# Blocks of x stored from ScalarE's queue, and the second unit's scores moved into the next pair, in a cross-attention and expert-FFN kernel

## Chip, core and metric

One core of one Trainium2 chip runs the whole program in one launch. The metric is the device time of one execution, in microseconds (us); lower is better. TensorE is PE, VectorE DVE, ScalarE ACT, GpSimd POOL and SyncE SP.

## What is computed

x has 32 sequences of 64 tokens with 512 features, 2048 tokens in all; the context has the same shape. Everything is float32.

```python
def attention(query, kv, Wq, bq, Wkv, bkv, Wo, bo):      # 32 query heads, 8 key/value heads, head width 128
    q = (query @ Wq + bq).reshape(B, L, 8, 4, 128)
    k, v = split(kv @ Wkv + bkv, 2, axis=-1)
    scores = einsum('blkgd,bmkd->bkglm', q, k) / sqrt(128)
    o = einsum('bkglm,bmkd->blkgd', softmax(scores), v)
    return o.reshape(B, L, 4096) @ Wo + bo
x = x + attention(layernorm(x), ctx, ...)
x = x + experts(layernorm(x))      # 8 experts of rank 16, the two best per token, softmax gates
```

## The kernel before

**Precision.** A float32 operand is split into a high part (a rounded copy, written by ACT) and a low part (the rest, a subtraction on POOL or DVE). A matrix product is three passes, high x high, low x high and high x low, on lines 1408 to 1410. So a high part always waits on ACT and a low part on POOL or DVE, before PE can use it.

**Start.** Keys and values of all heads are made in four steps. A step has 8 value tiles `V` and 8 key tiles `K`; PE fills a ring of four PSUM banks, DVE moves each tile to one of three slots (`SLOTS`) in `parts`, with a wait for the slot's earlier store, and SP stores it to `values_dram` or `keys_dram`. Between them PE transposes tiles of the context and of the normalised x. From x, ACT, DVE and POOL make seven blocks of 1 MB (`OPS`), which are operands of a seven-product scheme for x Wq (Strassen's, in Winograd's form), for each of two halves of the tokens, called duos 0 and 1 here. The blocks stand in `xo`, seven places, and `store_blocks` writes them to `x_dram`: duo 1's after step 1's first keys, duo 0's after step 3's, both from SP's queue, among the stores of keys. The stores share one counter, `blocks_stored`.

**Main part.** 16 pairs of units, `duo(g, p, first)`: for each of 8 key/value heads g, p = 0 and 1. A unit is 512 tokens for the four query heads of g. Per pair PE does 14 products (`product(g, p, k, r)`, six matmuls of 512 columns each, in the order k = 1, 6, 2, 7, 4, 5, 3), which DVE adds up to four tiles of queries (`y_sum`, `z_sum`, `w_sum`, `query_sum` for c11, c21, c22, c12); `scores` of both units, in chunks of four sequences; the softmax of each chunk, which goes to and fro: copy out of PSUM (ACT, `copy_half`), add and turn (DVE, `s_add`, `s_max`), peak swap (ACT, `swap_max`; DVE, `s_peak`), subtraction (POOL, `shift`), exponential (ACT), sum (DVE, ACT), scaling (POOL), turn back (DVE, `p_turn`), split (ACT, POOL). Then `outputs` (probabilities x values), and `out` (times Wo, added to `y`). `outputs` and `out` of a pair's units are done in the next pair. Pairs 2 to 13 are a hardware loop. Each engine's order is written out by hand in its own `duo`; engines meet at semaphores only.

**Places of blocks.** In the main part a pair's seven blocks share four places of `xo` (`BUF_OF`), because places 4 to 6 hold `oT` and `pT`, attention's own tiles. Before the first product of a block, PE waits for its load, `block_loaded`. SP issues `load_block(p, op, used)` when product `used` has released the place. In the first pair, blocks 4 to 6 are loaded again into places 2, 0 and 1. Blocks that the next pair needs first are loaded at the end of a pair.

**The first pair's joins.** ACT's `first_product` writes product 1 into `parts`, whose places were the stores' slots, so it waits until the last three stores of keys have landed. PE's first product waits until DVE has emptied the last key tile. `bo_bc`, the bias of the output, lies in `k_raw` until POOL's `residual` has added it to all 16 tiles of `y`; the first load of keys waits for that.

## Time and profile before

| what | value |
|---|---|
| median of 3 runs | 1111.5 us (1110.66 to 1112.6) |
| profiled execution's own time | 1111.75 us |
| its span in the trace | 1109.5 us |
| PE busy | 1045.1 us, 94% |
| DVE, POOL, ACT busy | 806.4, 675.6, 557.0 us |
| mean granted PE clock | 0.974 |

The time holds 2.25 us outside the span. Busy time of PE counts a matmul from its start to its modelled end. A granted clock of 1.00 is 2.4 GHz and 0.50 is 1.2 GHz.

### The profile page before, as it was taken

The page shows a single profiled execution, that of the slowest core. Times are in us where ns is not written, and L with a number is a line of the kernel's source. Part 1 is how long each engine was busy: PE and PEld are TensorE (multiplying, and loading weights), DVE is VectorE, ACT ScalarE, POOL GpSimd, SP SyncE. Part 2 cuts the span into 40 slices and gives each one's busy share as a digit, 9 for nine tenths or more (in the row PEclk, how much of TensorE's full clock was granted, in tenths as well). Part 3 has the DMA queues.
Part 4 walks back from the last instruction along what each step waited for, and adds up shares of the span by engine and source line. Part 5 has one row for each costly group of instructions (what it writes and reads, how often), then busy time and mean ns, then how long its engine had stood idle before and what let it go on. Part 6 is the DMA issues. An engine that isn't in the chain of part 4 may idle for free.

```text
span 1109.5 us, 17269 instructions
## 1 busy us (share of the span) xinstructions
PE 1045.1 (94%) x5389; PEld 856.0 (77%) x5389; DVE 806.4 (73%) x1420; ACT 557.0 (50%) x1314; POOL 675.6 (61%) x563
## 2 busy tenths in 40 slices
PE   7999799784999999999999999999999999997996
PEld 5887687664887887888788788878887888886884
DVE  4462346346897797789878877977887797788795
ACT  3132103225665665567566656756666665664320
POOL 1275125746786677578667867776786677674210
PEclk9999899986999999999999999999999999998998
DMA  8647753884727456372736446282736546240013
GB/s 303 191 123 277 235 180 105 328 299 149 294 93 259 145 201 233 113 286 92 284 127 222 179 170 240 101 299 102 261 122 228 182 167 243 102 149 10 1 40 113
DMA packets 86040, 201.12 MB, mean 181 GB/s; under 512 B 10560, under 2 KB 43368, under 8 KB 70384
## 3 DMA queue, kind: packets, MB, share of 16 engines
q1 hardware_dynamic: 86000, 200.61, 51.4%
q8 instruction: 23, 0.38, 0.1%
q14 instruction: 17, 0.14, 0.0%
HBM read 164.93 MB, written 35.65 MB: 181 GB/s over the span
## 4 chain that ended last, share of the span: by engine, by line
PE 58%; POOL 15%; DMA 9%; issue 8%; DVE 7%; SPq 1%; ACT 1%; POOLq 0%; DVEq 0%; ACTq 0%
PE banks L1408 17%; PE banks L1409 16%; PE banks L1410 16%; DMA xo<-x_dram 5%; POOL w_l L555 4%; DMA keys_dram<-parts 3%; PE banks L1543 3%; POOL qT_l L555 2%; POOL xo L555 2%; POOL low_or_x L588 2%; POOL low_or_x L581 2%; PE banks L1526 2%; PE banks L1527 2%; PE banks L1433 2%; SPq L411 1%
## 5 line engine op out<-in xcount | busy, mean ns | idle before, releaser
L555 POOL TENSOR_TENSOR qT_l<-parts,qT_h 128x512 fp32r<-128x512 f32 x128 | 165.3, 1296 | 63.6 <-ACT qT_h L725 63.5
L1408 PE MATMUL banks<-wo_h,xo 128*128 128x512 f32 x512 | 203.8, 398 | 0.0
L1409 PE MATMUL banks<-wo_l,xo 128*128 128x512 f32 x512 | 199.9, 391 | 0.0
L1410 PE MATMUL banks<-wo_h,xo 128*128 128x512 f32 x512 | 199.5, 390 | 0.0
L1408 PE MATMUL banks<-xo,w_h 128*128 128x512 f32 x448 | 181.4, 405 | 14.2 <-DVE parts L1008 11.0
L1409 PE MATMUL banks<-xo,w_h 128*128 128x512 f32 x448 | 177.3, 396 | 0.0
L1410 PE MATMUL banks<-xo,w_l 128*128 128x512 f32 x448 | 175.8, 393 | 0.0
L555 POOL TENSOR_TENSOR xo<-sT,xo 128x512 fp32r<-128x512 f32 (+1 forms) x72 | 102.2, 1420 | 76.9 <-ACT xo L725 76.9
L969 DVE TENSOR_TENSOR xo<-banks,xo 128x512 fp32r<-128x512 f32 (+1 forms) x156 | 100.7, 665 | 27.4 <-ACT xo L725 26.7
L1117 DVE SCALAR_TENSOR_TENSOR parts<-banks,g_bias,parts 128x512 f32<-128x512 f32 x128 | 95.0, 742 | 34.2 <-PE banks L1410 30.6
L588 POOL TENSOR_TENSOR low_or_x<-low_or_x,row_sum 128x512 f32<-128x512 f32 x64 | 70.7, 1104 | 74.3 <-DVE row_sum L1153 74.3
L1408 PEld LDWEIGHTS banks<-xo,w_h 128*128 128x128 f32 x448 | 85.2, 190 | 38.9 <-issue 17.0
L1408 PEld LDWEIGHTS banks<-wo_h,xo 128*128 128x128 f32 x512 | 96.1, 188 | 23.0
L1410 PEld LDWEIGHTS banks<-wo_h,xo 128*128 128x128 f32 x512 | 96.1, 188 | 20.9
L1409 PEld LDWEIGHTS banks<-wo_l,xo 128*128 128x128 f32 x512 | 96.2, 188 | 18.3
L725 ACT ACTIVATE qT_h<-parts 128x512 fp32r<-128x512 f32 x128 | 80.6, 630 | 58.5 <-DVE parts L1117 56.7
L725 ACT ACTIVATE xo<-banks 128x512 fp32r<-128x512 f32 (+1 forms) x156 | 85.0, 582 | 43.4 <-PE banks L1543 22.4
L1164 DVE TENSOR_TENSOR y<-banks,y 128x512 f32<-128x512 f32 x120 | 81.4, 683 | 33.5 <-PE banks L1410 33.0
L1410 PEld LDWEIGHTS banks<-xo,w_l 128*128 128x128 f32 x448 | 85.1, 190 | 19.0
L1409 PEld LDWEIGHTS banks<-xo,w_h 128*128 128x128 f32 x448 | 85.2, 190 | 15.4
L581 POOL TENSOR_TENSOR low_or_x<-low_or_x,row_max 128x512 f32<-128x512 f32 x64 | 70.5, 1101 | 42.7 <-DVE row_max L1139 41.9
L813 ACT COPY low_or_x<-banks 64x512 f32<-64x512 f32 x64 | 37.3, 583 | 116.5 <-PE banks L1527 116.4
(142 smaller groups left out, 2282.4 us busy)
## 6 DMA issues: line engine op xcount, KB each, us to landing
xo<-x_dram SPq DMA_DIRECT2D x108, 1024.0 KB, 6.9
x_dram<-xo SPq DMA_DIRECT2D x14, 1024.0 KB, 12.9
raw<-in_L_xattn_Wkv_dram SPq DMA_DIRECT2D x8, 1024.0 KB, 6.4
values_dram<-parts SPq DMA_DIRECT2D x64, 128.0 KB, 2.5
keys_dram<-parts SPq DMA_DIRECT2D x32, 256.0 KB, 2.8
raw<-in_L_xattn_Wq_dram SPq DMA_DIRECT2D x8, 1024.0 KB, 5.5
k_raw<-keys_dram SPq DMA_DIRECT2D x32, 256.0 KB, 4.7
raw<-in_L_xattn_Wo_dram SPq DMA_DIRECT2D x8, 1024.0 KB, 5.4
```

Of the source, the lines that this page charges most:

```text
L555: return nc.gpsimd.tensor_tensor(dst, src, high_part.bitcast(F32), ALU.subtract)
L581: nc.gpsimd.tensor_tensor(s[:, blocks, :], s[:, blocks, :], row_max[:, blocks].unsqueeze(2).broadcast_to([P, D // QR, QR]), ALU.subtract). ...
L588: nc.gpsimd.tensor_tensor(s[:, blocks, :], s[:, blocks, :], row_sum[:, blocks].unsqueeze(2).broadcast_to([P, D // QR, QR]), ALU.mult).then ...
L725: return nc.scalar.activation(dst, src, ACT.Copy)
L813: act.copy(half[L:P, c], att_s[L:P, :, 0, :])
L969: return nc.vector.tensor_tensor(dst, src, high_part.bitcast(F32), ALU.subtract)
L1117: nc.vector.scalar_tensor_tensor(out=slot_of(c, r), in0=product_of(d, p, k, r), scalar=q_bias(c, r), in1=slot_of(what, r), op0=ALU.add, op ...
L1164: nc.vector.tensor_tensor(y[:, t, :], ring[:, slot, :], y[:, t, :], ALU.add).then_inc(y_added, 1)
L1408: mm(dst, stat[0], mov[0], start=start, stop=False)
L1409: mm(dst, stat[0], mov[1], start=False, stop=False)
L1410: return mm(dst, stat[1], mov[0], start=False, stop=stop)
L1543: last = mm(turn[:, i, n % 2 * G * L:(n % 2 + 1) * G * L], v[keys_of, n, :], p[keys_of, n, :], start=p is pT_h and v is v_h, stop=p is pT_l)
```

## The change

Five edits, most of them for the pairs 0 and 1 only.

1. `store_blocks` moves from SP to ACT. Duo 1's seven stores are issued behind `split_wv(2)` in the start's order, duo 0's behind `split_q(0)`.
2. Pair 0 uses its seven blocks where they were made. SP no longer waits for the stores at its start, and loads none of blocks 4 to 6 for it; the wait for all 14 stores comes before the loads for pair 1. ACT waits for the stores before it writes `pT`.
3. `bo_bc` lies in `v_raw`. The first load of keys no longer waits for the residuals; the first load of values does, and POOL does tiles 3 and 7 later, inside pair 0.
4. The scores of pair 0's second unit move from its end into pair 1, on PE behind products 6 and 2. `outputs(0, ...)` move back behind product 4. On DVE the sums y of pair 1 move ahead to pair 0's end, and the second unit's softmax moves behind the sums c11 of pair 1. On ACT, `first_product` of pair 1 and `keys_high(1)` are moved ahead.
5. In all pairs with p = 0, the load of Wo (`load_wo`) is issued behind the loads of blocks 5, 4 and 6 and of the keys; before, it stood ahead of blocks 4 and 6.

```diff
@@ -186,7 +186,7 @@
         x_copy = parts[:, 5, :].rearrange("p (c n) -> p c n", c=KC)
-        bo_bc = k_raw.rearrange("p b l -> p (b l)")
+        bo_bc = v_raw.rearrange("p n d -> p (n d)")
         sT = sb("sT", [P, 2 * D])
@@ -402,13 +402,6 @@
                 load_w(step, wkv_v, NKV * HD + step % CHUNKS * D)
-
-            def store_blocks(duo, pairs_done):
-
-                sp.wait_ge(diff_low, pairs_done)
-                sp.wait_ge(tile_emptied, tile_no["x", DUO_TILES[pairs_done - 1][1]] + 1)
-                for op in range(OPS):
-                    sp.dma_start(x_dram[duo, op], xo[:, op].rearrange("p s k n -> p (s k n)").bitcast(F32)).then_inc(blocks_stored, 16)
@@ -437,10 +430,6 @@
                             load_w(STEPS, wq_v, 0)
-                        if name[1] == 1:
-                            store_blocks(1, 4)
-                        if name[1] == STEPS - 1:
-                            store_blocks(0, 8)
                 if name[0] == "c" and 4 <= name[1] < PTILES:
@@ -490,18 +479,16 @@
                 if first:
-                    sp.wait_ge(blocks_stored, 16 * DUOS * OPS)
+                    for m in range(len(kv_order) - SLOTS, len(kv_order)):
+                        sp.wait_ge(kv_stored[m % SLOTS], kv_value[m])
                 else:
                     load_values(g if p else g - 1, 2 * p - 1 if p else UNITS - 1, 2 * d - 1)
-                load_block(p, 5, product(1))
+                    load_block(p, 5, product(1))
+                    load_block(p, 4, product(6))
+                    load_block(p, 6, product(2))
+                load_keys(g, 2 * p + 1, 2 * d + 1)
                 if p == 0:
                     load_wo(wo_v[:, bass.ds(g * G, G), :], QLOWS + OPS * g + OPS)
-                load_block(p, 4, product(6))
-                if first:
-                    for m in range(len(kv_order) - SLOTS, len(kv_order)):
-                        sp.wait_ge(kv_stored[m % SLOTS], kv_value[m])
-                load_block(p, 6, product(2))
-                load_keys(g, 2 * p + 1, 2 * d + 1)
                 if p == 1 and last_group:
@@ -512,16 +499,19 @@
                     load_w(STEPS + g + 1, wq_v, (g + 1) * (G * HD))
+                if first:
+                    sp.wait_ge(blocks_stored, 16 * DUOS * OPS)
                 if not last:
...
                     load_block(1 - p, 2, product(5))
+                if first:
+                    sp.wait_ge(resid_ready, TILES)
                 load_values(g, 2 * p, 2 * d)
...
-            sp.wait_ge(resid_ready, TILES)
             m = kv_no["K", 0, 0, 0]
@@ -642,6 +632,9 @@
                 query_low(d, "c11", 1)
+                if first:
+                    residual(3)
+                    residual(7)
                 query_low(d, "c21", 0)
@@ -698,7 +691,7 @@
             split_q(0, list(USE_OF), True)
-            for t in (0, 4, 1, 5, 2, 6, 3, 7):
+            for t in (0, 4, 1, 5, 2, 6):
                 residual(t)
@@ -765,6 +758,13 @@
+            def store_blocks(duo, pairs_done):
+
+                act.wait_ge(diff_low, pairs_done)
+                act.wait_ge(tile_emptied, tile_no["x", DUO_TILES[pairs_done - 1][1]] + 1)
+                for op in range(OPS):
+                    act.dma_start(x_dram[duo, op], xo[:, op].rearrange("p s k n -> p (s k n)").bitcast(F32)).then_inc(blocks_stored, 16)
+
             def first_product(d, p, r):
@@ -841,9 +842,13 @@
                 wo_high_part(0)
-                first_product(d, p, 0)
-                keys_high(2 * d)
-                first_product(d, p, 1)
+                if second:
+                    copy_half(1, 1)
+                    keys_high(2)
+                else:
+                    first_product(d, p, 0)
+                    keys_high(2 * d)
+                    first_product(d, p, 1)
                 if not first:
@@ -878,6 +883,8 @@
                 copy_half(2 * d, 1)
+                if first:
+                    keys_high(1)
                 swap_max(2 * d, 0)
@@ -885,12 +892,17 @@
                 exponents(2 * d, 0)
-                keys_high(2 * d + 1)
+                if not first:
+                    keys_high(2 * d + 1)
                 if not first:
...
                 exponents(2 * d, 1)
+                if first:
+                    first_product(1, 1, 0)
+                    first_product(1, 1, 1)
+                    act.wait_ge(blocks_stored, 16 * DUOS * OPS)
                 if split:
@@ -900,7 +912,7 @@
                 probs_high(2 * d, 1)
-                if not last:
+                if not first and not last:
                     copy_half(2 * d + 1, 1)
@@ -918,7 +930,10 @@
                         split_wv(name[1] + 1)
+                    if name[1] == 1:
+                        store_blocks(1, 4)
             split_q(0, list(USE_OF), True)
+            store_blocks(0, 8)
             duo(0, 0, True)
@@ -1183,15 +1199,21 @@
                     s_peak(2 * d - 1, 0)
-                y_sum(d, p, 0)
-                if not first:
-                    s_max(2 * d - 1, 1)
-                y_sum(d, p, 1)
-                if not first:
-                    s_sum(2 * d - 1, 0)
-                    s_peak(2 * d - 1, 1)
+                if not second:
+                    y_sum(d, p, 0)
+                    if not first:
+                        s_max(2 * d - 1, 1)
+                    y_sum(d, p, 1)
+                    if not first:
+                        s_sum(2 * d - 1, 0)
+                        s_peak(2 * d - 1, 1)
                 query_sum(d, p, "c11", 0)
                 query_sum(d, p, "c11", 1)
+                if second:
+                    s_add(1, 1)
+                    s_max(1, 1)
+                    s_sum(1, 0)
+                    s_peak(1, 1)
                 if not first:
@@ -1253,12 +1275,15 @@
                     combine_w(g + 1, 4, False)
+                if first:
+                    y_sum(1, 1, 0)
+                    y_sum(1, 1, 1)
                 s_add(2 * d + 1, 0)
...
                 add(7)
-                if not last:
+                if not first and not last:
                     s_add(2 * d + 1, 1)
@@ -1479,12 +1504,10 @@
                 first, second = isinstance(d, int) and d == 0, isinstance(d, int) and d == 1
-                buf = BUF_OF[op]
+                buf = op if first else BUF_OF[op]
                 if r == 0:
-                    if op >= XBUFS:
-                        pe.wait_ge(block_loaded[buf], d * 32 + 16)
-                    elif not first:
-                        pe.wait_ge(block_loaded[buf], d * 16 if buf == 3 else d * 32)
+                    if not first:
+                        pe.wait_ge(block_loaded[buf], d * 32 if op >= XBUFS else d * 16 if op == 3 else d * 32 - 16)
                     if p == 0:
@@ -1563,16 +1587,24 @@
                 product(g, p, 6, 1)
-                if not first:
+                if second:
+                    scores(0, 1, 0)
+                elif not first:
                     outputs(2 * d - 2, 0)
...
                 product(g, p, 2, 1)
+                if second:
+                    scores(0, 1, 1)
                 product(g, p, 7, 0)
...
                 product(g, p, 4, 0)
-                if not first:
+                if second:
+                    outputs(0, 0)
+                elif not first:
                     outputs(2 * d - 2, 1)
                 product(g, p, 4, 1)
+                if second:
+                    outputs(0, 1)
                 product(g, p, 5, 0)
@@ -1589,10 +1621,12 @@
                 out(5)
-                scores(d, 1, 0)
+                if not first:
+                    scores(d, 1, 0)
                 out(6)
                 out(7)
-                scores(d, 1, 1)
+                if not first:
+                    scores(d, 1, 1)
```

What the edits do to the engines' orders is seen in three places. First SP, in step 1 of the start: one piece of the difference in SP's rows. `keys_dram<-parts` are the stores of keys, `x_dram<-xo` those of the blocks, `raw<-in_L_xattn_Wkv_dram` a load of weights.

```order
 L401 DMA keys_dram<-parts 128x512 x2
 L376 DMA raw<-in_L_xattn_Wkv_dram 128x4x512
-L411 DMA x_dram<-xo 128x2048 x7
 L401 DMA keys_dram<-parts 128x512 x6
 L388 DMA y<-in_x_dram 128x512 x4
```

ACT in the same step, after the change. `w_h<-raw` is `split_wv(2)`, `qT_h<-banks` are high parts of context tiles 8 to 13, `wo_h<-raw` the next split of weights.

```order
L718 ACTIVATE w_h<-raw 128x512 x4
L766 DMA x_dram<-xo 128x2048 x7
L718 ACTIVATE qT_h<-banks 128x4x128 x6
L718 ACTIVATE wo_h<-raw 128x512 x4
L718 ACTIVATE qT_h<-banks 128x4x128 x2
```

The seven stores left SP's row, where six stores of keys stood behind them, and stand on ACT ahead of the context tiles.

Second SP in pair 0, before the change. `k_raw<-keys_dram` loads keys, `raw<-in_L_xattn_Wo_dram` is `load_wo`, `xo<-x_dram` loads blocks, `v_raw<-values_dram` values.

```order
L411 DMA x_dram<-xo 128x2048 x7
L401 DMA keys_dram<-parts 128x512 x6
L468 DMA k_raw<-keys_dram 128x512
L480 DMA xo<-x_dram 128x2048
L380 DMA raw<-in_L_xattn_Wo_dram 128x4x512
L480 DMA xo<-x_dram 128x2048 x2
L468 DMA k_raw<-keys_dram 128x512
L480 DMA xo<-x_dram 128x2048 x2
L475 DMA v_raw<-values_dram 64x4x128 x2
L480 DMA xo<-x_dram 128x2048 x2
L468 DMA k_raw<-keys_dram 128x512
```

And after it:

```order
L401 DMA keys_dram<-parts 128x512 x6
L457 DMA k_raw<-keys_dram 128x512 x2
L380 DMA raw<-in_L_xattn_Wo_dram 128x4x512
L469 DMA xo<-x_dram 128x2048 x2
L464 DMA v_raw<-values_dram 64x4x128 x2
L469 DMA xo<-x_dram 128x2048 x2
L457 DMA k_raw<-keys_dram 128x512
```

The three loads of pair 0's own blocks 5, 4 and 6 are gone, and both units' keys come ahead of every block.

Third DVE in pair 1, before the change: the two sums y (L1094), the softmax of unit 1's second chunk (L1132, L1134) and sum of its first (L1145), the sums c11 (L1117), the low parts of unit 0's first outputs (L969), and then the sums z (L1102).

```order
L1094 TENSOR_TENSOR parts<-banks,parts 128x512
L1132 STREAM_TRANSPOSE low_or_x<-sT 128x512
L1134 TENSOR_REDUCE row_max<-low_or_x 128x16
L1094 TENSOR_TENSOR parts<-banks,parts 128x512
L1145 TENSOR_REDUCE row_sum<-low_or_x 128x16
L1139 TENSOR_TENSOR row_max<-row_max,other 128x16
L1117 SCALAR_TENSOR_TENSOR parts<-banks,g_bias,parts 128x512 x2
L969 TENSOR_TENSOR xo<-banks,xo 128x2x4x64 x2
L1150 TENSOR_TENSOR row_sum<-row_sum,other 128x16
L1153 RECIPROCAL row_sum<-row_sum 128x16
L1102 TENSOR_TENSOR parts<-banks,parts 128x512 x2
```

After it, with the lines' new numbers (L1132 is `query_sum`, L1141 and L1142 `s_add`, L984 the low parts of outputs, L1117 z):

```order
L1132 SCALAR_TENSOR_TENSOR parts<-banks,g_bias,parts 128x512 x2
L1141 TENSOR_TENSOR sT<-banks,low_or_x 64x512
L1142 TENSOR_TENSOR sT<-banks,low_or_x 64x512
L1147 STREAM_TRANSPOSE low_or_x<-sT 128x512
L1149 TENSOR_REDUCE row_max<-low_or_x 128x16
L1160 TENSOR_REDUCE row_sum<-low_or_x 128x16
L1154 TENSOR_TENSOR row_max<-row_max,other 128x16
L984 TENSOR_TENSOR xo<-banks,xo 128x2x4x64 x2
L1165 TENSOR_TENSOR row_sum<-row_sum,other 128x16
L1168 RECIPROCAL row_sum<-row_sum 128x16
L1117 TENSOR_TENSOR parts<-banks,parts 128x512 x2
```

The addition of the second chunk's halves stood at pair 0's end and now stands between c11 and z, and the sums y left for pair 0's end.

## Rows read from the trace of the kernel before

**Rows 1.** The page: PE's busy share, and its granted clock in 40 slices.

```profile
PE 1045.1 (94%) x5389; PEld 856.0 (77%) x5389; DVE 806.4 (73%) x1420; ACT 557.0 (50%) x1314; POOL 675.6 (61%) x563
...
PEclk9999899986999999999999999999999999998998
```

**Rows 2.** Waits of the whole span, PE's: total us, times, longest.

```profile
PE banks L1408 <- DVE parts L1008: 11.0, 1, 11.0
PE banks L1433 <- DVE qT_l L969: 10.9, 2, 10.2
```

**Rows 3.** Stretches: length, busy of PE, PEld, DVE, ACT, POOL, clock, DMA, GB/s.

```profile
100.00:110.00 10.00, 8.42 (x41) 6.60 (x39) 0.69 (x1) 2.92 (x6) 9.77 (x8) 1.00 1.00 424
...
220.00:230.00 10.00, 3.15 (x8) 2.51 (x9) 2.88 (x4) 0.00 (x0) 7.48 (x7) 0.50 0.81 282
```

**Rows 4.** Timeline of SP's queue: start, length in us, then what it issued.

```profile
92.85 4.72 SPq L411 DMA_DIRECT2D x_dram<-xo  x7
97.61 23.09 SPq L401 DMA_DIRECT2D keys_dram<-parts  x6
...
202.87 6.61 SPq L411 DMA_DIRECT2D x_dram<-xo  x7
```

**Rows 5.** DMA of 80 to 130 us: times issued, size, median us to landing.

```profile
x_dram<-xo SPq DMA_DIRECT2D x7, 1024.0 KB, 13.9
keys_dram<-parts SPq DMA_DIRECT2D x8, 256.0 KB, 3.3
```

**Rows 6.** Timelines of ACT, DVE and PE around the first stall, idle time in brackets.

```profile
99.04 2.20 ACT L725 ACTIVATE w_h<-raw 128x512 fp32r<-128x512 f32 x4 [9.94 <-DMA raw<-in_L_xattn_Wkv_dram]
...
105.70 0.60 ACT L725 ACTIVATE qT_h<-banks 128x512 fp32r<-128x512 f32 x1 [2.61 <-PE banks L1433]
...
117.08 0.75 DVE L1008 TENSOR_SCALAR parts<-banks,bias 128x512 f32<-128x512 f32 x1 [14.64 <-DMA keys_dram<-parts]
...
118.58 1.09 PE L1433 MATMUL banks<-ident,y 128*128 128x128 f32 x4 [10.16 <-DVE qT_l L969]
```

**Rows 7.** The chain that ended last, one step a row, behind the first stall.

```profile
119.66 0.43 PE banks L1408
...
123.15 0.23 PE banks L1408
```

**Rows 8.** Timeline of PE, the last key product and the waits in pairs 0 and 1.

```profile
215.43 0.39 PE L1410 MATMUL banks<-qT_h,wo_l 128*128 128x512 f32 x1
...
226.85 0.76 PE L1408 MATMUL banks<-xo,w_h 128*128 128x512 f32 x1 [11.03 <-DVE parts L1008]
...
251.66 0.36 PE L1526 MATMUL banks<-qT_h,kT 128*128 128x256 f32 x1 [1.39 <-DVE sT L1127]
...
260.65 0.55 PE L1526 MATMUL banks<-qT_h,kT 128*128 128x256 f32 x1 [7.81 <-POOL kT L555]
...
267.46 0.55 PE L1526 MATMUL banks<-qT_h,kT 128*128 128x256 f32 x1 [4.75 <-DVE sT L1127]
...
286.87 0.39 PE L1408 MATMUL banks<-xo,w_h 128*128 128x512 f32 x1
```

**Rows 9.** Timeline of ACT: last weight split, pair 0's copies and keys, last exponential.

```profile
211.64 0.63 ACT L725 ACTIVATE w_h<-sT 128x512 fp32r<-128x512 f32 x1
230.80 0.59 ACT L773 COPY parts<-banks 128x512 f32<-128x512 f32 x1 [18.52 <-DMA keys_dram<-parts]
232.15 0.63 ACT L725 ACTIVATE kT<-k_raw 128x512 fp32r<-128x512 f32 x1 [0.77 <-DMA k_raw<-keys_dram]
...
261.59 0.63 ACT L823 ACTIVATE low_or_x<-low_or_x 128x512 f32<-128x512 f32 x1 [0.84 <-POOL low_or_x L581]
```

**Rows 10.** Waits of PE from 320 to 1060 us.

```profile
PE banks L1408 <- DMA xo<-x_dram: 2.7, 6, 0.5
```

**Rows 11.** Timeline of SP's queue in pair 2.

```profile
328.70 0.41 SPq L380 DMA_DIRECT2D raw<-in_L_xattn_Wo_dram  x1
329.61 0.81 SPq L480 DMA_DIRECT2D xo<-x_dram  x2
```

More of the change, by code:

```diff
@@ L832, in duo @@
                 split, last = p == 1 and not last_group, p == 1 and last_group
+                second = isinstance(d, int) and d == 1
                 def wo_high_part(c):
@@ L1175, in duo @@
                 split, last = p == 1 and not last_group, p == 1 and last_group
+                second = isinstance(d, int) and d == 1
                 def add(j):
@@ L1549, in duo @@
                 d = g * DUOS + p
+                second = isinstance(d, int) and d == 1
                 def out(j):
```

## The prediction

> **What bounds the kernel now.** I read the page first. PE is busy 94% of the span, no other engine over 73%, so only time in which PE stands still, or runs at the lower clock, can be won. The row of granted clock is 9 in nearly all slices and dips in two places, at about 110 and 220 to 280 us [rows 1]. The list of PE's waits names them: 11.0 us for DVE's eviction at L1008, and 10.2 us for DVE's low part of a context tile [rows 2]. Stretches of 10 us show what goes on there: DMA is full, 424 GB/s, and then PE stands at clock 0.50 [rows 3]. SP's queue says what fills it: seven stores of x blocks from 92.85 us and seven from 202.87, each time with the key stores behind them [rows 4]. A block store lands after 13.9 us, a key store usually after 3.3 [rows 5]. Behind the blocks DVE waits 14.64 us for a slot, and PE 10.16 for DVE [rows 6]. So both large stalls are of one kind: a small store behind 7.34 MB in the same queue, 17.2 us at 427 GB/s.
>
> Between pairs 0 and 1 PE waits for other things: 1.39, 7.81 and 4.75 us for scores of pair 0, whose softmax and keys have no other matmuls to hide behind [rows 8]. In the loop only six waits for a block are left, 2.7 us [rows 10].
>
> **First place: stores of step 1.** PE lost 10.16 us [rows 6] and ran on at half clock: seven steps of the chain take 0.43 us in place of 0.23, 1.4 us, and the four transposes ahead of them 0.6 more [rows 7]. That is 12.2 us. Now the key stores don't stand behind the blocks. What is new is that ACT issues. Its weight split ends at 101.24 [rows 6], and seven issues took SP 4.72 us [rows 4], so ACT is free at 105.96. High part 0.60 and low part 0.69 of the first context tile end at 107.3. PE wanted to turn the third tile, which needs that bank, at 105.07 (its high part began at 105.70, behind 0.60 of transposes [rows 6]): a new wait of 2.3. No row shows what an issue costs on ACT. Below, it is nothing, and the wait too; above, 6.61 us as SP's second time [rows 4], and the wait is 4.2. I take SP's first, since that queue was empty too. Value stores and the next weight load then run beside the blocks up to about 125 us. PE has a ring of four banks and DVE three slots between; I allow 0.7, with 0 and 3 as ends. Gain 12.2 - 2.3 - 0.7 = **9.2** (5 to 12.2).
>
> **Second place: stores of step 3, pairs 0 and 1.** I count from the last key product's end, 215.82, to product 5 of pair 1 at 286.87, 71.0 us [rows 8]. In it PE does 24 products of six matmuls at 0.2285 (1.37 each, 32.9), four score chunks of 1.0 and two `outputs` of 0.95: 38.8. Waits are 11.03, 0.48 (a block), 1.39, 7.81 and 4.75, 25.5 together. The rest, 6.7, is low clock behind them.
>
> Now the same stretch anew, by durations from the trace. DVE empties the last key tile at 216.7: 1.0 wait. Four products run to 222.4. Product 2 needs ACT's copy of product 1, and that the last key store. Before, copy, keys and copy ran from 230.80 to 233.26, 4.1 us behind that store's eviction [rows 9]. Now the blocks share the DMA engines with it, so I add 1 to 2 us; the first load of keys comes behind it and must land before ACT reaches the second copy, about 226.3. PE's second half of product 2 would start at 223.8: **2.5** (0 to 5). Eight more products bring the scores of chunk 0 at 237.3; POOL, with two residuals of 1.23 in between, has the low parts at 236.0, no wait. Chunk 1 waits for `s_add` of chunk 0 as before, 1.4, and ends at 242.1. Stores of blocks, from 212.3 [rows 9], need 17.2 us plus some 2.4 MB of other transfers, so they are done at about 235; block 0 of pair 1 lands at about 241.5. It is just in time.
>
> Then pair 1, in its new order. Products 1 and 6 end at 247.6. Scores of unit 1 need the keys' low part, which POOL does behind shift and c12: 248.8, **1.3**. Product 2 needs the copy on ACT, now behind the second exponential. Before, that ended at 262.22 [rows 9], 9.4 us behind chunk 1's end at 252.84; keys are split earlier now, so 8.5, and the copy is there at 251.2: **1.3**. Chunk 1 of unit 1 waits for `s_add`, behind an inverse and two sums y on DVE: **2.7**. Product 4 waits 0.3 for c11. The second `outputs` waits until DVE has the first's low parts, which now stand behind `s_add`, `s_max`, sum and peak of unit 1, with two turns to ACT between them: 267.9, **3.5**; z is 0.8 behind. New waits: 1.0 + 2.5 + 1.4 + 1.3 + 1.3 + 2.7 + 0.3 + 3.5 + 0.8 = 14.8. 38.8 + 14.8 = 53.6, against 71.0: 17.4 won. PE's next scores then wait 1.3 more for POOL's c21. Gain **16.1**; the chain's joints of 1 to 3 us each, and the copy's bounds, give 9 to 22.
>
> **Third place: load of Wo.** In pair 2 it went out at 328.70, when `w_l` was finished, and blocks 4 and 6 behind it, at 329.61 [rows 11]. Product 6 had released block 4's place at about 326. Now block 4 goes 3 us earlier and the wait of 0.40 to 0.50 in each of six pairs is gone, **2.6** (2 to 2.7). Wo goes out at about 331, and is wanted 39 us later: covered. The other waits of SP move with it; keys are out at 331 as before. If Wo were to collide with blocks 0 and 2 at 336, it costs nothing, since they are wanted in the next pair.
>
> **Free.** The bias in `v_raw`: the values' load now waits for POOL's last residual at 233, and is issued behind blocks at 236. Wait for all stores on ACT: 235 against 251.
>
> **Sum.** 9.2 + 16.1 + 2.6 = 27.9. From the profiled execution's 1111.75 (span 1109.5 and 2.25 around it) that leaves 1083.9, and 1083.6 from the median, which is 0.25 lower.
>
> **A rule against it.** Rows 4 and 5 show small stores late behind large ones of one queue; they can't show two queues. The Trainium skill, page "DMA: Bandwidth & Descriptors", section "Issuing engines are not separate DMA queues", says that transfers started by several engines run on the same 16 DMA engines, and that spreading saves issue time only. Its section "Queues, rings and completion order" gives SP and ACT a ring each on every DMA engine, served in turn by the packet. No run here shows either yet. By the second, the sum stands; by the first, read strictly, it is the first rival.
>
> **Rivals.** *One line for both queues* (12%). Key stores issued behind the blocks still land behind them. In step 1 they mostly don't matter: the blocks now go out at 101 rather than 93, and three slots and a ring of four carry PE until 119, so the 9.2 stay. At pair 0, the last key store would land at 231, the second copy be done at 234.5, and PE would lose 8 us and 2 of clock more: 1093.6. For it: 13.9 us for each block at full bandwidth [rows 5]. Against it: nothing yet.
>
> *ACT is held until the blocks have gone* (4%). An issue then takes 2.4 us, ACT stays until 118 and 229. The first place loses 2 in place of winning 9, the second wins 10: 1101. Against it: SP issued seven in 4.72 us while they took 17 to move [rows 4].
>
> *The waits of pair 1 don't come* (8%), as engines make up for them: 14.8 shrinks to 5, and the first place gives all 12.2. Together with the loop's 2.6 that is 40.7: 1071.
>
> *Slower* (3%): low clock throughout pairs 0 and 1. The new waits are many and short, where the old were few and long. If PE were granted 1.2 GHz from 242 to 292 us, each of its 180 matmuls costs 0.43 in place of 0.23 [rows 7]: 36 us, more than the 27.9, for 1120. It turns to a loss from 140 matmuls on. Against it: the clock came back within 12 matmuls after 226.85, and a wait of 1.39 at 251.66 [rows 8] was followed by full clock.
>
> **Numbers.** The forecast has 70%; 3% are for something that undoes the gain elsewhere. The likeliest case's own bounds give gains from 5 + 9 + 2 = 16 to 12.2 + 22 + 2.7 = 37, 1075 to 1095. The range, 1072 to 1098, takes in the first rival and the edge of the third, and leaves out the other 15 in 100. A measurement of this kernel tells 0.2% from no change. Chances: faster 0.93, within 0.2% 0.03, slower 0.04.
>
> **What would show it.** PE's waits at L1408 for DVE and at the context tile fall from 11.0 and 10.2 to under 4 each. The key stores land within 6 us while blocks are under way. ACT shows a gap of about 5 us ahead of the first context tile of step 2. No wait for a block in pairs 2 to 12. Pair 1 has five or six waits of 1 to 4 us ahead of product 5. I am wrong if key stores land after 10 us or more, if block 0 of pair 1 comes late by over 3 us, or if the granted clock stays low past 245 us.

## The result, and the profile after

| what | before | after |
|---|---|---|
| median in one group of runs | 1112.05 us (1110.66 to 1113.71, 4 runs) | 1094.24 us (1093.7 to 1095.01, 4 runs) |
| ratio to before, 95% interval | 1 | 0.984 (0.9823 to 0.9857) |
| span of the profiled execution | 1109.5 us | 1092.8 us |
| mean granted PE clock | 0.974 | 0.983 |

The changed kernel is 17.8 us faster; the forecast was 27.9 faster, 1083.6. The time lies in the range (1072 to 1098), and direction and places are as forecast. Of three terms the middle one is much too large. Of the 10.6 us to the forecast, 0.5 come from the median before, 1112.05 where the forecast started from 1111.5. (One more group of runs, e12 below, gave 1095.88 for the same kernel: between groups, differences are uncertain by some 1.6 us.)

The page of the changed kernel, its busy row, its row of granted clock, and the queues. q1 is SP's, q10 is new and ACT's.

```profile
PE 1044.5 (96%) x5389; PEld 856.2 (78%) x5389; DVE 805.2 (74%) x1420; ACT 556.5 (51%) x1314; POOL 674.9 (62%) x563
...
PEclk9999999898999999999999999999999999998998
...
q1 hardware_dynamic: 83552, 182.78, 48.4%
q10 hardware_dynamic: 2016, 14.68, 3.3%
```

Against [rows 1] PE's work is the same 1045 us; what was won is idle time. In the row of clock the dip at 110 us has gone; that at 220 to 280, an 8 and a 6 before, is now an 8 at 191 to 219 and an 8 at 246 to 273 us.

**First place.** Timelines of ACT and PE there: start, length, engine, line, what; idle time and its releaser in brackets.

```profile
100.79 5.12 ACTq L766 DMA_DIRECT2D x_dram<-xo  x4
105.96 1.08 ACT L718 ACTIVATE qT_h<-banks 128x512 fp32r<-128x512 f32 x2 [5.33 <-issue]
...
128.35 2.19 ACT L718 ACTIVATE wo_h<-raw 128x512 fp32r<-128x512 f32 x4 [10.06 <-DMA raw<-in_L_xattn_Wkv_dram]
...
107.43 0.63 PE L1458 MATMUL banks<-ident,y 128*128 128x128 f32 x4 [1.66 <-DVE qT_l L984]
...
131.80 0.50 PE L1433 MATMUL banks<-w_h,qT_h 128*128 128x512 f32 x1 [2.25 <-DVE qT_l L984]
```

ACT stands 5.33 us issuing, as forecast, and PE waits 1.66 in place of 10.16 [rows 6]. The second row of PE is new: PE waits 2.25 us at 131.80, since the weights of the next step land late. SP issued them only at 117.68, behind the key stores and four loads of x tiles that ran beside the blocks; the blocks themselves had gone by 122.

**Second place.** Timelines of PE, DVE, ACT and SP's queue from the last key product to product 5 of pair 1, to set beside [rows 8, 9]. L1023 empties key tiles, L773 copies product 1.

```profile
208.19 0.39 PE L1435 MATMUL banks<-qT_h,wo_l 128*128 128x512 f32 x1
213.72 0.77 PE L1433 MATMUL banks<-xo,w_h 128*128 128x512 f32 x1 [5.15 <-DVE parts L1023]
...
223.87 0.47 PE L1433 MATMUL banks<-xo,w_h 128*128 128x512 f32 x1 [2.12 <-ACT parts L773]
227.32 0.50 PE L1433 MATMUL banks<-xo,w_h 128*128 128x512 f32 x1 [1.82 <-ACT parts L773]
242.23 0.35 PE L1549 MATMUL banks<-qT_h,kT 128*128 128x256 f32 x1 [1.40 <-DVE sT L1142]
251.72 0.36 PE L1549 MATMUL banks<-qT_h,kT 128*128 128x256 f32 x1 [2.83 <-issue]
...
253.91 0.77 PE L1433 MATMUL banks<-xo,w_h 128*128 128x512 f32 x1 [1.01 <-ACT parts L773]
270.37 0.58 PE L1566 MATMUL banks<-xo,v_h 64*128 64x256 f32 x2 [2.97 <-DVE xo L984]
272.26 0.77 PE L1433 MATMUL banks<-xo,w_h 128*128 128x512 f32 x1 [0.25 <-DVE parts L1117]
...
212.83 0.75 DVE L1023 TENSOR_SCALAR parts<-banks,bias 128x512 f32<-128x512 f32 x1 [6.11 <-DMA keys_dram<-parts]
...
204.44 6.95 ACTq L766 DMA_DIRECT2D x_dram<-xo  x7
223.14 0.59 ACT L773 COPY parts<-banks 128x512 f32<-128x512 f32 x1 [18.14 <-DMA keys_dram<-parts]
226.16 0.63 ACT L718 ACTIVATE kT<-k_raw 128x512 fp32r<-128x512 f32 x1 [2.44 <-DMA k_raw<-keys_dram]
...
213.98 14.60 SPq L457 DMA_DIRECT2D k_raw<-keys_dram  x2
```

From the last key product's end, 208.57, to product 5 at 272.26 are 63.7 us, in place of 71.0. The waits sum to 17.6, the work is the same 38.8, and 7.3 are left, nearly all of it for matmuls at 1.2 GHz (durations of 0.77 and 0.63 in place of 0.39). Three waits at the front, 9.1 us, hang on transfers: DVE can't empty the last key tile until a slot's store has landed, ACT can't copy until the last key store has, and ACT's second copy stands behind the keys, landed at 226.1. No row shows a wait for a block.

What the two queues moved in that stretch, 206 to 222 us: each queue's packets, MB and share of the 16 engines' time; then times issued, size, median us to landing.

```profile
q10 hardware_dynamic: 749, 5.48, 84.5%
q1 hardware_dynamic: 575, 1.05, 17.2%
...
x_dram<-xo ACTq DMA_DIRECT2D x5, 1024.0 KB, 13.3
keys_dram<-parts SPq DMA_DIRECT2D x3, 256.0 KB, 10.3
k_raw<-keys_dram SPq DMA_DIRECT2D x1, 256.0 KB, 12.2
```

**Loop.** The copy of a group's bias on DVE stands once in each pass of two pairs; the first and the sixth after it, in the changed kernel.

```profile
310.67 0.17 DVE L1198 COPY g_bias<-bias 128x4 f32 x1
...
902.59 0.17 DVE L1198 COPY g_bias<-bias 128x4 f32<-128x4 f32 x1
```

### The profile page after: what moved, and what is told of

The parts are those of the page before. It is cut to its first block, busy times and chain, and to the rows that moved or that the text cites. A ratio compares the mean times of both kernels' runs of the same rounds, so it can differ in the third digit from the quotient of the medians.

```text
span 1092.8 us, 17254 instructions
## 1 busy us (share of the span) xinstructions
PE 1044.5 (96%) x5389; PEld 856.2 (78%) x5389; DVE 805.2 (74%) x1420; ACT 556.5 (51%) x1314; POOL 674.9 (62%) x563
## 4 chain that ended last, share of the span: by engine, by line
PE 83%; DVE 6%; DMA 5%; ACT 2%; POOL 2%; issue 1%; SPq 1%; ACTq 1%; DVEq 0%
PE banks L1433 25%; PE banks L1434 23%; PE banks L1435 23%; PE banks L1566 5%; PE banks L1550 3%; PE banks L1549 3%; DMA raw<-in_L_xattn_Wkv_dram 2%; PE banks L1458 1%; DMA k_raw<-keys_dram 1%; DMA keys_dram<-parts 1%; DMA raw<-in_L_xattn_Wq_dram 1%; ACTq L766 1%; SPq L388 0%; POOL wo_l L545 0%; DVE stats L1059 0%
## 5 line engine op out<-in xcount | busy, mean ns | idle before, releaser
L984 DVE TENSOR_TENSOR xo<-banks,xo 128x512 fp32r<-128x512 f32 (+1 forms) x156 | 100.7, 665 | 28.7 <-ACT xo L718 28.1
L1132 DVE SCALAR_TENSOR_TENSOR parts<-banks,g_bias,parts 128x512 f32<-128x512 f32 x128 | 94.9, 742 | 30.3 <-PE banks L1435 27.9
L1435 PEld LDWEIGHTS banks<-xo,w_l 128*128 128x128 f32 x448 | 85.7, 191 | 19.2
```

What stands on the lines that cost most here:

```text
L984: return nc.vector.tensor_tensor(dst, src, high_part.bitcast(F32), ALU.subtract)
L1132: nc.vector.scalar_tensor_tensor(out=slot_of(c, r), in0=product_of(d, p, k, r), scalar=q_bias(c, r), in1=slot_of(what, r), op0=ALU.add, op ...
L1435: return mm(dst, stat[1], mov[0], start=False, stop=stop)
```

## The experiments

Every kernel was timed in turns with the kernel before. Medians of the kernel before were 1111.88 us (e1 to e4), 1110.61 (e5 to e8) and 1111.94 (e9 to e12).

**e1, late stores.** The changed kernel, with pair 0's seven stores issued on ACT behind its two copies of product 1:

```diff
                     first_product(d, p, 1)
+                    if first:
+                        store_blocks(0, 8)
...
             split_q(0, list(USE_OF), True)
-            store_blocks(0, 8)
```

> The kernel after the change, with pair 0's seven block stores issued on ACT behind pair 0's two copies of product 1, so that the last key stores and the first load of keys no longer run beside them. Sharing theory (small transfers are served in turn with the 8 KB rows of the blocks and land after about 10 us in place of 3.5, and this sets PE's start of pair 0): the last key store lands within 4 us, the waits of 5.15, 2.12 and 1.82 us at pair 0's products shrink to under 3 together and product 2 starts 8 us sooner; block 0 of pair 1 then comes some 4 us late, so the net gain is 3 to 6 us, 1088 to 1091. Clock theory (what the second place lost is the granted clock of 0.5 after each wait): waits may move but low clock stays, 1093 to 1095.

Measured 1088.35 us (1087.53 to 1090.22), ratio 0.9791 (0.9775 to 0.9807). DMA from 200 to 232 us, and PE's waits:

```profile
keys_dram<-parts SPq DMA_DIRECT2D x4, 256.0 KB, 2.5
raw<-in_L_xattn_Wo_dram SPq DMA_DIRECT2D x1, 1024.0 KB, 19.2
...
209.36 0.47 PE L1434 MATMUL banks<-xo,w_h 128*128 128x512 f32 x1 [1.01 <-DVE parts L1024]
...
229.67 0.58 PE L1550 MATMUL banks<-qT_h,kT 128*128 128x256 f32 x1 [2.36 <-POOL qT_l L545]
...
242.79 0.80 PE L1434 MATMUL banks<-xo,w_h 128*128 128x512 f32 x1 [7.08 <-DMA xo<-x_dram]
```

The three front waits shrink from 9.1 to 1.0 us, with key stores landing in 2.5 us: the blocks beside them made the waits. Product 2's second half begins 7.9 us behind the last key product, in place of 18.75. About half of these 10.8 us is given back (5.8 are left at the first pass's bias copy): PE waits 2.36 us for POOL, and since the stores now end later, pair 1's block 0 comes 7.08 us late.

**e2, filled wait.** The changed kernel with 22 matmuls on idle data ahead of pair 0's first product:

```diff
             pe.wait_ge(diff_low, 8)
+            for _ in range(22):
+                mm(turn[:, 0, :], wo_h[:, 0, 0:P], cT[0][0][:, 0, :], start=True, stop=True)
             duo(0, 0, True)
```

> The kernel after the change, with 22 extra matmuls of 512 columns (5.0 us at full clock) into a free bank, in the wait ahead of pair 0's first product; their result is never read. They keep PE busy so that the granted clock stays high. Clock theory: pair 0's first 16 matmuls run at 0.23 in place of 0.43 us each, 3.4 us won, 1091. Sharing theory: the copy of product 1 waits for the last key store whatever PE does, so the products only wait longer at product 2: same as the change, 1094 within 1.

Measured 1094.61 us (1093.29 to 1095.72), ratio 0.9848 (0.9832 to 0.9865): nothing. The first products ran at full clock (granted 1.00 from 206 to 214 us), and then PE waited for the copy, 4.37 us in place of 2.12:

```profile
222.62 0.76 PE L1433 MATMUL banks<-xo,w_h 128*128 128x512 f32 x1 [4.37 <-ACT parts L773]
```

**e3, spread stores.** The changed kernel with duo 1's seven stores issued one each behind context tiles 8 to 14.

```diff
                 if name[0] in "cx":
                     tile_high(name)
+                    if name[0] == "c" and 8 <= name[1] < 8 + OPS:
+                        store_blocks(1, 4, [name[1] - 8])
...
-                    if name[1] == 1:
-                        store_blocks(1, 4)
```

> The kernel after the change, with duo 1's seven stores issued one by one on ACT, each behind the high part of one of the context tiles 8 to 14, in place of seven in a row. Sharing theory: ACT no longer stands 5.3 us ahead of the first context tile, small stores meet fewer blocks, and PE's waits of 1.66 and 2.25 us go: 2 to 4 us won, 1090 to 1092. Rival (the order of the tiles' splits, not the stores, sets these waits): 1094.

Measured 1094.12 us (1091.19 to 1096.34), ratio 0.9832 (0.9814 to 0.985): nothing either. ACT no longer stands, the 1.66 us are gone, but the next weights come only 1.1 us sooner than in the changed kernel, and PE waits for them, 3.89 us where the two waits made 3.91:

```profile
127.26 0.63 ACT L718 ACTIVATE wo_h<-raw 128x512 fp32r<-128x512 f32 x1 [11.70 <-DMA raw<-in_L_xattn_Wkv_dram]
...
130.70 0.80 PE L1433 MATMUL banks<-w_h,qT_h 128*128 128x512 f32 x1 [3.89 <-DVE qT_l L984]
```

**e4, Wo's load alone.** The kernel before with edit 5 only (`load_wo` behind `load_keys` for p = 0).

```diff
                 load_block(p, 5, product(1))
-                if p == 0:
-                    load_wo(wo_v[:, bass.ds(g * G, G), :], QLOWS + OPS * g + OPS)
                 load_block(p, 4, product(6))
...
                 load_keys(g, 2 * p + 1, 2 * d + 1)
+                if p == 0:
+                    load_wo(wo_v[:, bass.ds(g * G, G), :], QLOWS + OPS * g + OPS)
```

> The kernel before the change with the fifth edit alone, Wo's load behind the loads of blocks 5, 4 and 6 and of the keys. If only the wait for block 4 was to be won, 2.7 us: 1109.3. By the length of a loop pass in the two traces (99.4 us before, 98.65 after) 0.74 in each of six passes, 4.4 us: 1107.6.

Measured 1105.81 us (1104.65 to 1106.11), ratio 0.9947 (0.993 to 0.9963): 6.1 us, more than expected. The kernel before, with DVE's bias copy of the first and of the sixth pass after it, and PE at one of its six waits:

```profile
323.10 0.17 DVE L1182 COPY g_bias<-bias 128x4 f32 x1
...
919.54 0.17 DVE L1182 COPY g_bias<-bias 128x4 f32<-128x4 f32 x1
...
335.98 0.39 PE L1410 MATMUL banks<-xo,w_l 128*128 128x512 f32 x1
336.76 0.49 PE L1408 MATMUL banks<-xo,w_h 128*128 128x512 f32 x1 [0.40 <-DMA xo<-x_dram]
337.10 0.40 PE L1409 MATMUL banks<-xo,w_h 128*128 128x512 f32 x1
```

And e4:

```profile
320.63 0.17 DVE L1182 COPY g_bias<-bias 128x4 f32 x1
...
912.55 0.17 DVE L1182 COPY g_bias<-bias 128x4 f32<-128x4 f32 x1
```

A pass took (919.54 - 323.10) / 6 = 99.41 us and takes 98.65: 0.75 for a wait that is listed with 0.40 to 0.50. Idle time is counted from the matmul's modelled end, 336.37, but the next one would have started at 336.21, 0.23 behind the last start; and the one behind it follows after 0.34, not 0.23. So the wait costs 0.40 + 0.16 + 0.11 = 0.67, and nearly all of the 0.75 is found. Six passes give 4.5; the wait of 0.48 in pair 0 went too. Of the last 1 us, this profile shows where it lies: e4's last key product ends 1.1 us earlier than before (214.71, before 215.82), where the edit changes nothing. That much is a difference between executions.

**e5, queue alone.** The kernel before with edit 1 only: `store_blocks` on ACT, nothing else.

> The kernel before with edit 1 alone: both groups of block stores from ScalarE's queue, all else as before. My theory: the queue is the larger part of the gain. The first place gives what it gave in the changed kernel, 7.3 us; at pair 0 the last key store lands about 10 us after its issue rather than 18.5, so product 2 starts some 6 us sooner, but pair 0 still loads three blocks again, behind all stores, so PE waits for block 5 (product 4) or loses it again: 2 to 6 of it stay. 1099 to 1103 us. Rival: the queue is worth the first place only and all of the second comes from the blocks used in place and the moved scores: 1104 to 1106 us.

Measured 1107.06 us (1106.18 to 1108.89), ratio 0.9965 (0.9948 to 0.9981), 3.5 us: less than either theory. PE in pair 0:

```profile
214.08 0.77 PE L1407 MATMUL banks<-xo,w_h 128*128 128x512 f32 x1 [5.08 <-DVE parts L1007]
...
228.66 0.50 PE L1407 MATMUL banks<-xo,w_h 128*128 128x512 f32 x1 [3.44 <-ACT parts L769]
239.29 0.50 PE L1407 MATMUL banks<-xo,w_h 128*128 128x512 f32 x1 [3.54 <-DMA xo<-x_dram]
```

The first place's gain is there (the last key product ends at 209.0, before at 215.8). Then pair 0 waits 13.0 us in four pieces, where it waited 11.5 in two: its first keys and its block 5 queue behind everything else. From the last key product to the first pass's bias copy (319.4) are 110.4 us, before 107.3: by itself, the move costs pairs 0 and 1 3.1 us.

**e6, without edit 4.** The changed kernel with the second unit's scores at pair 0's end, as before.

> The changed kernel without edit 4: the second unit's scores at pair 0's end as before, the other four edits kept. Waits of the kernel before for these scores (7.8 and 4.75 us) come back in part, since the keys are now loaded and split earlier; edit 4's own new waits in pair 1 (2.83, 1.01, 2.98, 0.25 us in the changed kernel) and their low clock go. My theory: the reorder is worth 4 to 6 us: 1098 to 1100 us. Rival: the moved scores only shift waits from pair 0 to pair 1, worth under 1.5 us: 1094 to 1096 us.

Measured 1098.15 us (1097.51 to 1098.48), ratio 0.9889 (0.9872 to 0.9905). The waits of 7.80 and 4.75 us [rows 8] are back whole:

```profile
251.26 0.55 PE L1531 MATMUL banks<-qT_h,kT 128*128 128x256 f32 x1 [7.80 <-POOL kT L545]
258.06 0.55 PE L1531 MATMUL banks<-qT_h,kT 128*128 128x256 f32 x1 [4.75 <-DVE sT L1133]
```

Its bias copy of the first pass is at 313.8 us, in the changed kernel at 310.7, and in the second profile of that (e12) at 311.7. Edit 4 removes 12.5 us of waits and is worth 2 to 4: the rest it pays for by waits in pair 1 (7.1 us) and the low clock behind them. From the last key product to that copy e6 takes 104.9 us, the changed kernel 102.1. So in this stretch the queue alone costs 3.1 us (e5), edits 2, 3 and 5 together win 5.5 (e6 against e5), and edit 4 wins 2.8. Edits 2 and 3 have no run of their own.

**e7, own counter.** e1, with the stores of blocks 0 and 2 first and on a semaphore of their own; pair 1's loads of these two wait for it alone.

```diff
                 if first:
-                    sp.wait_ge(blocks_stored, 16 * DUOS * OPS)
+                    sp.wait_ge(early_stored, 32)
                 if not last:
                     load_block(1 - p, 0, product(4))
                     load_block(1 - p, 2, product(5))
+                if first:
+                    sp.wait_ge(blocks_stored, 16 * (DUOS * OPS - 2))
...
```

> The kernel with the late stores (pair 0's seven stores behind its two copies of product 1), and the stores of blocks 0 and 2 go first and count on a semaphore of their own, so that pair 1's loads of blocks 0 and 2 wait for those two only. In the late kernel PE lost 7.08 us for block 0, since its load waited for all seven. My theory: the wait was made by the shared counter; it falls under 1 us, and the time to 1082 to 1084 us. Rival: the DMA engines are full until the seven stores, Wo's 1 MB and the two loads have moved, whatever the order, and block 0 or 1 still comes 4 us late or more: 1086 to 1088 us.

Measured 1087.91 us (1087.41 to 1089.37), ratio 0.9799 (0.9783 to 0.9816), as e1: my theory falls, the rival holds. The loads went out at 222.65 in place of 237.97, but behind Wo's 1 MB in one queue, beside the stores in the other, and PE waited as long:

```profile
raw<-in_L_xattn_Wo_dram SPq DMA_DIRECT2D x1, 1024.0 KB, 20.0
...
241.42 0.80 PE L1437 MATMUL banks<-xo,w_h 128*128 128x512 f32 x1 [7.13 <-DMA xo<-x_dram]
```

**e8, weights first.** e7, with step 3's first weights issued ahead of four loads of x tiles.

> The same kernel with one more move: step 3's first load of weights is issued ahead of four 256 KB loads of x tiles, not behind them. In the changed kernel these weights landed 10 us after ScalarE was ready for them and PE then waited 2.25 us. My theory: the weights land 2 to 3 us sooner, that wait goes, 2 to 3 us less than the kernel without this move. Rival: the load shares the DMA engines with the seven block stores either way and the x tiles come late instead: no difference beyond 1 us, or slower.

Measured 1086.93 us (1085.3 to 1088.45), ratio 0.9791 (0.9775 to 0.9807). The wait of 2.1 us at 131 is gone in its profile, and the last key product ends 1.4 us sooner; the intervals of e7 and e8 overlap, so the gain is likely but not settled.

**e9, order of loads.** e8, with pair 1's blocks 0 and 2 loaded ahead of Wo, as soon as pair 0's first two products have released their places.

```diff
                 load_keys(g, 2 * p + 1, 2 * d + 1)
+                if first:
+                    sp.wait_ge(early_stored, 32)
+                    load_block(1, 0, product(1))
+                    load_block(1, 2, product(6))
                 if p == 0:
                     load_wo(wo_v[:, bass.ds(g * G, G), :], QLOWS + OPS * g + OPS)
...
```

> The kernel with late stores, own counter for blocks 0 and 2 and the weights moved in step 3; now SyncE also issues pair 1's loads of blocks 0 and 2 ahead of Wo's 1 MB, as soon as their two stores have landed (their places are free after pair 0's first two products, since pair 0 uses its blocks in place). My theory: block 0 was late because 11 MB had to move ahead of it at 400 GB/s; with Wo and five stores no longer ahead of it, it lands before PE wants it, and the 6.1 us go. About half comes back as waits for pair 1's scores (2.8 us for the keys' low part, 1.0 for the copy), as in the changed kernel: 1083 to 1084 us against 1086.9. Rival: all of it comes back, since the softmax of pair 0 sets the pace in pair 1: 1086 to 1087 us.

Measured **1083.07 us** (1082.57 to 1083.46), ratio 0.9737 (0.9723 to 0.975), the fastest of all: 12.8 us less than the changed kernel in the same group of runs. PE no longer waits for block 0 (6.13 us in e8). Block 2, for product 6, comes 1.09 us late, and block 1, for product 2, 3.36:

```profile
237.21 0.50 PE L1441 MATMUL banks<-xo,w_h 128*128 128x512 f32 x1 [1.09 <-DMA xo<-x_dram]
...
246.14 0.66 PE L1441 MATMUL banks<-xo,w_h 128*128 128x512 f32 x1 [3.36 <-DMA xo<-x_dram]
```

**e10, two stores early.** e9, with the stores of blocks 0 and 2 at the changed kernel's place again, ahead of the last key stores, and five behind the copies.

> The same, with the stores of blocks 0 and 2 issued at the changed kernel's place, behind the last split of weights, and only the other five behind the two copies. Between 205 and 214 us the DMA engines were at 60 to 280 GB/s, so 2 MB fit there in part. My theory: the two blocks are loaded 3 to 5 us sooner, the last key store lands 1 to 2 us later (at 4 us after its issue, from 2.5): 0 to 1 us to either side of the kernel without the split. Rival: 2 MB ahead of the last key store hold it up as seven did in the changed kernel (9.8 us): 3 to 5 us slower.

Measured 1088.17 us (1086.5 to 1089.16), ratio 0.9784 (0.9771 to 0.9798): 5.1 slower than e9, the rival. Key stores land after 6.5 us, and the first product waits 3.92 us in place of 1.01:

```profile
keys_dram<-parts SPq DMA_DIRECT2D x5, 256.0 KB, 6.5
...
210.63 0.77 PE L1442 MATMUL banks<-xo,w_h 128*128 128x512 f32 x1 [3.92 <-DVE parts L1032]
```

The blocks did come sooner, since pair 1 has no wait for a block left, and the kernel is slower all the same. It takes two blocks, not seven, to hold up what PE waits for.

**e11, filled waits in pair 1.** The changed kernel with 22 and 7 small matmuls around unit 1's first scores.

```diff
                 if second:
-                    scores(0, 1, 0)
+                    for n in range(29):
+                        mm(turn[:, 0, 0:2 * P], w_h[:, 6, 1, 0:P], w_h[:, 6, 0, :], start=True, stop=True)
+                        if n == 21:
+                            scores(0, 1, 0)
```

> The changed kernel with 29 matmuls of 256 columns added in pair 1 on data that is at hand, 22 ahead of unit 1's first scores and 7 behind them, where PE waited 2.83 and 1.01 us; their result isn't used. Granted clock from 252 to 262 us was 0.60 to 0.70 in the changed kernel. Theory of the low clock: with PE busy through both waits the clock stays up there, 2.5 to 3.5 us less. Rival: the products behind those waits are held by DVE and ACT, not by PE's speed, so that faster products wait again (the later wait of 2.98 us grows): within 1 us of the changed kernel.

Measured 1094.21 us (1092.49 to 1095.14), ratio 0.9835 (0.9822 to 0.9849), 1.7 less than e12. Stretches of 256 to 262 and 274 to 280 us (columns as in [rows 3]; the granted clock stands right behind POOL's busy time):

```profile
256.00:262.00 6.00, 3.54 (x18) 2.80 (x17) 5.41 (x9) 2.77 (x6) 3.74 (x4) 0.91 0.59 184
...
274.00:280.00 6.00, 6.00 (x26) 4.43 (x24) 5.30 (x10) 4.45 (x11) 6.00 (x5) 1.00 0.60 191
```

and in e12:

```profile
256.00:262.00 6.00, 6.00 (x21) 4.49 (x20) 5.22 (x9) 2.98 (x7) 3.75 (x4) 0.60 0.50 143
...
274.00:280.00 6.00, 6.00 (x19) 4.74 (x19) 5.05 (x9) 4.60 (x11) 6.00 (x6) 0.67 0.51 167
```

The clock did stay up at 256 us, and it bought nothing there: a wait of 2.46 for `s_add` took the time, and product 5 came 30.1 us behind pair 0's last scores in both (272.76 - 242.67 and 273.19 - 243.15). What was won, was won behind product 5, where PE has no one to wait for. So the rival holds for the first low stretch, the theory for the second, at about half its price.

**e12, the changed kernel again.**

> The changed kernel itself once more, to stand beside the other three on one chip. 1094.2 us, as before: within 0.1% of it. If it differs by more, the differences between kernels of different groups of runs are uncertain by that much.

Measured 1095.88 us (1095.53 to 1097.13), ratio 0.9856 (0.9841 to 0.9871). It differs from the first group's by 0.15%, more than the 0.1% expected, so differences across groups are uncertain by some 1.6 us.

## Why the prediction was right in direction and 10.6 us too far

| term | forecast | measured | read from |
|---|---|---|---|
| first place | 9.2 | 7.3 | end of last key product, 215.82 to 208.57 |
| second place | 16.1 | 5.2 | from there to the first pass's bias copy, 107.3 to 102.1 |
| loop | 2.6 | 4.5 | 0.75 in each of six passes |

17.0 together, of 16.7 in the spans; the tail gives back 0.3.

**First place, right, 1.9 too high.** ACT was free at 105.96, to the digit as forecast, but by luck: I had all seven issues behind the weight split, for 4.72 us. Three went out during the split, which began 0.6 earlier, and the other four took 5.12. PE's wait was 1.66 (2.3). The 0.7 that I allowed for the weights behind the blocks was 2.25, and before the place this execution already ran about 0.5 later; some 0.5 stay open. e3 shows that ACT's issues cost nothing in the end: without them, PE waits the same time for the weights.

**Second place: the failed step.** It is the sentence "Now the blocks share the DMA engines with it, so I add 1 to 2 us", and with it copy 2 "about 226.3". I took the share as if the small store would take a third longer. It lost most of it. The same mistake is in the step before, "DVE empties the last key tile at 216.7: 1.0 wait": I put no time at the tile's slot, which must be free of its earlier key store. DVE waited 6.11 us for that, and PE 5.15. Of the 5.6 us by which the front waits exceed the forecast, this one has 4.15 and the two copies 1.4.

From 206 to 222 us q10 moved 5.48 MB in 749 packets and q1 1.05 MB in 575: 7.3 KB a packet against 1.8. The queues seem to take turns, but a turn of the one is four times the other's, and q1 was left with 66 GB/s of 408. At that rate a key store of 256 KB takes 4.0 us, up to three are under way (three slots), and each landed after about 10 us; the keys' load behind them took 12.2. Product 2's second half, counted from the last key product, began at 18.75 us in place of 10.5: 8.3 us late. e1 took the blocks away from there and the front waits fell by 8.1 us; e10 put two of seven back and lost 5.1. So it is shown that blocks beside the key stores make these waits.

That turns are taken packet by packet is only read from the counts, and was not tested by another packet size. In the first place, from 101 to 118 us, the counts are 856 against 402 packets, less even; whether q1 then had something queued all the time, no run shows. The Trainium skill, page "DMA: Bandwidth & Descriptors", section "Queues, rings and completion order", says that each DMA engine serves its queues in turn, a packet at a time; 749 against 575 roughly agrees. The strict reading of the section "Issuing engines are not separate DMA queues" on the same page of the Trainium skill, that a second issuing engine saves issue time only, does not hold here, since the key stores landed after 10.3 us beside 7.34 MB that needed 18 at 408 GB/s.

**The number alone would have misled.** The rival *one line for both queues* gave 1093.6, and 1094.2 was measured. Its mechanism is refuted: key stores didn't land behind the blocks. The true case lies between it and mine, and that its time was hit within 1 us is chance. *ACT is held* is refuted too: seven issues took 6.95 us, not 17. Pair 1's waits did come, and the clock was not low throughout (1.00 from 222 to 252 us).

**Low clock, forecast 0, was 7.3 us in the stretch.** I had 53.6 us for it, it took 63.7: 2.8 more waits (5.6 more at the front, 2.8 fewer behind) and 7.3 of low clock. But by e2 and e11 little of that is lost, since products at half speed ran into time in which they would have waited. Adding waits and low clock up, as I did for before, overstates both. What the low clock does cost is mostly behind product 5: from there to the first bias copy it is 38.4 us, 36.2 before, 2.2 given back, though the 1.3 that I had there for POOL's c21 did not come; e11 won 1.5 there.

**Pair 1's joints, right as a sum, not one by one.** 11.3 forecast (all but the first two waits), 8.5 measured: 1.40 (1.4), 2.83 for the keys' low part (1.3), 1.01 for the copy (1.3), none for `s_add` (2.7), 2.97 for the outputs (3.5), 0.25 for z (0.8). POOL does the keys behind one more low part of queries than I had placed ahead of them.

**Loop, mechanism right, size off.** The listed idle time, 0.45, isn't the loss, 0.75 (e4).

**What I named as signs.** ACT's gap, no wait for a block from pair 2 on, and the context tile's wait came as forecast. The first product's wait was 5.15 and not under 4, the key stores landed after 10 us and not 6, and pair 1 had three waits of 1 to 4 us ahead of product 5, not five or six. Of my three signs of being wrong, one came in full: key stores that land after 10 us or more. Block 0 was in time. The clock was back at 1.00 by 245 us but fell again, to 0.60 and 0.70 from 252 to 262, which I had not foreseen.

## What to carry to other kernels

Put a large transfer on a second queue to get it out of the way of small ones, but time it too: while it runs, small transfers land late all the same, so it belongs behind the last of them that an engine waits for, and then what is loaded next goes out in the order in which it is wanted (e9, which holds the moves of e1, e7 and e8 too: 12.8 us more than the change itself gave). Before counting on a share of bandwidth, look at MB and packets of each queue. A wait costs more than its idle time where matmuls overlap, and a low clock costs less than its matmuls' extra time where the next thing waits for another engine anyway.

## What the runs showed of the hardware that I had not expected

- Two queues that were both busy got unequal bandwidth, here roughly by their packets' size: 84.5% of the engines' time for 7.3 KB packets, 17.2% for 1.8 KB ones. In e1, Wo's load of 1 MB took 19.2 us beside block stores, and 6.3 in the changed kernel, issued at 228.62 when they had landed.
- ACT issues a single DMA in 0.33 to 0.35 us, in e3 also while blocks were moving, but seven of 1 MB in a row took 6.95 us at 204 us and four 5.12 at 100.79. The activations behind them in ACT's order had to wait for the last issue (5.33 us idle).
- ACT issued its first store at 98.61, while its weight split had just begun (98.44 to 100.63): these issues did not wait for the activations ahead of them to end.
- A PE wait listed with 0.40 us cost 0.75 in each pass.
